# Sharing the blockwise FP4 rounding of two weight matrices between VectorE and GpSimd, beside an attention

## The reference

```python
def fp4_quant_dequant(x):                      # blocks of 16 along the last dim
    xb = x.reshape(shape[:-1] + (shape[-1] // 16, 16))
    scale = jnp.maximum(jnp.max(jnp.abs(xb), -1, keepdims=True) / 6.0, 1e-12)
    idx = jnp.searchsorted(_MID, jnp.abs(xb / scale))
    return (_GRID[idx] * jnp.sign(xb) * scale).reshape(shape)
gate = fp4_linear(x, w_gate); y = fp4_linear(x, w_up)
h = silu(gate) * y;           out = fp4_linear(h, w_down)
```

## Time and profile before

| | |
|---|---|
| median of three runs | 1594.88 us (1593.48 to 1599.5) |
| the profiled execution | 1599.5 us, its span 1597.7 us |
| busy over the span | PE 1452.7, DVE 711.7, ACT 496.5, POOL 430.0 us |
| mean granted TensorE clock | 0.934 |

### The profile page before, as it was taken

One profiled execution on the slowest core, in us unless ns is written; L12 is line 12 of the kernel. 1 busy time (PEld: TensorE's weight loads), 2 busy tenths in 40 slices (PEclk: granted clock), 3 DMA queues, 4 the chain that ended last, 5 costly groups with the idle time before them and its releaser, 6 DMA issues. The chain is left out here.

```text
span 1597.7 us, 26548 instructions
## 1 busy us (share of the span) xinstructions
PE 1452.7 (91%) x11152; PEld 1066.0 (67%) x11152; DVE 711.7 (45%) x1289; ACT 496.5 (31%) x824; POOL 430.0 (27%) x252
## 2 busy tenths in 40 slices
PE   7788987577997999999999999999999998898995
PEld 3565875243543778878878788787887876334873
DVE  2355259999524433232332323323233232675832
ACT  0313312141111204324343242432534344332602
POOL 6102010046314033313133131331313211224921
PEclk9778967788997999999999999999999999899997
DMA  6300030010201421111111011110111113203000
GB/s 246 124 35 1 1 145 1 0 73 1 79 0 60 136 75 42 54 38 47 54 37 54 31 54 54 35 55 28 59 54 35 47 39 148 106 0 125 1 1 26
DMA packets 49141, 88.01 MB, mean 55 GB/s; under 512 B 28536, under 2 KB 41088, under 8 KB 45952
## 3 DMA queue, kind: packets, MB, share of 16 engines
q1 hardware_dynamic: 49024, 86.32, 15.4%
HBM read 76.61 MB, written 9.70 MB: 54 GB/s over the span
## 5 line engine op out<-in xcount | busy, mean ns | idle before, releaser
L1151 POOL TENSOR_TENSOR ctx_hi<-ctx_raw,one 128x1536 fp32r<-128x1536 f32 (+1 forms) x32 | 91.5, 2858 | 568.7 <-DMA ctx_raw<-in_ctx 365.6
L1349 ACT COPY ET<-PS 128x512 f32<-128x512 f32 (+1 forms) x224 | 129.6, 584 | 279.8 <-PE PS L1253 204.9
L1452 DVE TENSOR_SCALAR_CACHE_REDUCE E<-PS 128x384 f32<-128x384 f32 (+1 forms) x256 | 131.8, 571 | 178.8 <-PE PS L1230 178.2
L1421 DVE TENSOR_TENSOR V<-PS,vbias 128x512 f32<-128x512 f32 (+1 forms) x104 | 71.7, 691 | 195.1 <-PE PS L1197 195.0
L1197 PE MATMUL PS<-wv_lo,ctx_hi 128*128 128x512 f32 (+1 forms) x416 | 128.4, 409 | 0.0
L1197 PE MATMUL PS<-ctx_raw_r,wk_hi 128*128 128x384 f32 (+1 forms) x512 | 128.2, 355 | 0.0
L1253 PE MATMUL PS<-ident,E 128*128 128x128 f32 (+1 forms) x832 | 123.7, 274 | 1.1 <-issue 1.1
L1356 ACT ACTIVATE E<-E,peak 128x1601 f32<-128x1601 f32 x64 | 103.5, 1623 | 66.9 <-DVE peak L1457 66.9
L1197 PE MATMUL PS<-wv_hi,ctx_hi 128*128 128x512 f32 (+1 forms) x416 | 121.3, 413 | 0.8 <-issue 0.8
L1197 PE MATMUL PS<-ctx_hi,wk_hi 128*128 128x384 f32 (+1 forms) x512 | 120.5, 357 | 0.0
L1154 POOL TENSOR_TENSOR ctx_raw_r<-ctx_raw,ctx_hi 128x1536 fp32r<-128x1536 f32 (+1 forms) x32 | 116.8, 3651 | 2.5
(11 more groups left out here) (289 smaller groups left out, 2289.9 us busy)
## 6 DMA issues: line engine op xcount, KB each, us to landing
ctx_raw<-in_ctx SPq DMA_DIRECT2D x24, 768.0 KB, 4.3
ctx_raw<-in_ctx_first SPq DMA_DIRECT2D x8, 900.0 KB, 4.6
rel_scr<-rel_out SPq DMA_DIRECT2D x8, 640.0 KB, 3.6
fwk<-in_fwk SPq DMA_DIRECT2D x1, 4096.0 KB, 12.2
fwv<-in_fwv SPq DMA_DIRECT2D x1, 4096.0 KB, 13.7
corr<-rel_scr SPq DMA_DIRECT2D x64, 48.0 KB
p_scr<-E SPq DMA_DIRECT2D x16, 192.0 KB, 2.3
near<-p_scr SPq DMA_DIRECT2D x64, 48.0 KB
```

Of the source, the lines that this page charges most:

```text
L1151: nc.gpsimd.tensor_tensor(ctx_hi[r][:, :, 0:n], ctx_raw[r][:, :, 0:n], one[:].unsqueeze(1).broadcast_to([P, KC, n]), ALU.mult).then_inc(S[ ...
L1349: nc.scalar.copy(ET[0:n, j % ET_RING, :], src[0:n, :]).then_inc(S["et_out"], 1)
L1421: v.tensor_tensor(V[0:rows, at % V_RING, :], bank(4 + NUMBER[unit] % 2)[0:rows, :], vbias[0:rows, :], ALU.add).then_inc(S["v_out"], 1)
L1452: v.tensor_scalar(E[:, p, k0:k0 + n], bank(r)[:, 0:n], 1.0, None, ALU.mult, ALU.max, accum_out=tops[:, p, c:c + 1]).then_inc(S["s_out"], 1)
```

## The change

The rounding is divided anew. DVE keeps the maxima, the scales and the division (now with the sign unchanged). The maximum with GRID becomes an operation of its own on `grid` (`floor`); then POOL, in a new `pool`, computes q + grid and q - grid, and for the first 8 of the 16 chunks (`BY_POOL`) the product with the scale as well. For the other 8 chunks DVE takes that product (`join_by_vector`). DVE waits, before the division of chunk n, for chunk n - 4 to be joined, by whichever engine. POOL's part stands between its four bias additions and its norm steps. ACT's part is as it was.

```diff
--- before.py
+++ after.py
@@ -396,7 +396,7 @@
                     residual(t - 1)
                 other(2)
             if beside:
-                beside.finish(dve, ch)
+                beside.finish(dve)
 
             dve.wait_ge(p_ready, NT)
             for t in range(NT - 1):
@@ -433,6 +433,8 @@
         def _(pool):
             for t in range(NT):
                 nc.gpsimd.tensor_tensor(s.X[:, t, :], s.X[:, t, :], s.bias[out_bias][:], ALU.add).then_inc(xb_ready, 1)
+            if beside:
+                beside.pool(pool)
             for t in range(NT):
                 nm.pool(pool, t)
 
@@ -612,17 +614,20 @@
 
     WIDTH = INNER // 2
     CHUNKS = 2 * IC * D // WIDTH
+    BY_POOL = CHUNKS // 2
     STAGES = 4
     GRID = 2.0 ** 22 + 1.0
 
     def __init__(self, nc, sem, region, s):
-        self.nc, self.s, self.started, self.measured = nc, s, 0, 0
+        self.nc, self.s, self.started, self.measured, self.floored, self.joined = nc, s, 0, 0, 0, self.BY_POOL
         nb = self.WIDTH // BLOCK
         self.q = [region.tensor(f"fp4w_q{r}", [P, self.WIDTH]) for r in range(self.STAGES)]
         self.grid = [region.tensor(f"fp4w_grid{r}", [P, self.WIDTH]) for r in range(self.STAGES)]
         self.scale = [region.tensor(f"fp4w_scale{r}", [P, 2, nb]) for r in range(self.STAGES // 2 + 1)]
         self.inverse = region.tensor("fp4w_inverse", [P, 2, nb])
-        self.divided, self.sized = sem("fp4w_divided"), sem("fp4w_sized")
+        self.divided, self.sized, self.ready, self.rounded, self.done = (
+            sem("fp4w_" + n) for n in ("divided", "sized", "ready", "rounded", "done"))
+        self.joined_dve = sem("fp4w_joined_dve")
 
     def chunk(self, n):
         w = self.s.w["wg" if n < self.CHUNKS // 2 else "wu"][:].rearrange("p r n -> p (r n)")
@@ -632,44 +637,57 @@
     def scale_of(self, n):
         return self.scale[n // 2 % len(self.scale)][:, n % 2]
 
+    def wait_joined(self, eng, n):
+
+        if n < self.BY_POOL:
+            eng.wait_ge(self.done, n + 1)
+        else:
+            eng.wait_ge(self.joined_dve, n - self.BY_POOL + 1)
+
     def vector(self, dve, ch, count):
 
         v = self.nc.vector
         for n in range(self.started, min(self.started + count, self.CHUNKS), 2):
             if n % (self.CHUNKS // 2) == 0:
                 dve.wait_ge(self.s.loaded["wg" if n == 0 else "wu"], 16)
+            if n >= 2 * len(self.scale):
+                for k in range(2):
+                    self.wait_joined(dve, n + k - 2 * len(self.scale))
             for k in range(2):
                 ch.add(v.tensor_reduce(self.scale_of(n + k), self.chunk(n + k), AX.X, ALU.max, apply_absolute_value=True))
             ch.sync()
             sc, inv = self.scale[n // 2 % len(self.scale)][:], self.inverse[:]
             ch.link(v.tensor_scalar(sc, sc, float(np.float32(1 / 6)), 1e-12, ALU.mult, ALU.max))
             ch.link(v.reciprocal(inv, sc))
-            ch.link(v.tensor_scalar(inv, inv, -(1.0 - 2.0 ** -23), None, ALU.mult))
+            ch.link(v.tensor_scalar(inv, inv, 1.0 - 2.0 ** -23, None, ALU.mult))
+            self.floor(dve, n)
+            self.join_by_vector(dve, n - 2)
             for k in range(2):
+                if n + k >= self.STAGES:
+                    self.wait_joined(dve, n + k - self.STAGES)
                 v.tensor_tensor(blocks(self.q[(n + k) % self.STAGES][:]), self.chunk(n + k),
                                 inv[:, k].unsqueeze(2).broadcast_to([P, self.WIDTH // BLOCK, BLOCK]), ALU.mult).then_inc(self.divided, 1)
             self.started = n + 2
-            if n >= 2:
-                self.complete(dve, ch, n - 2)
-
-    def complete(self, dve, ch, n):
-
-        v, pair = self.nc.vector, (n, n + 1)
-        q, grid = (lambda k: self.q[k % self.STAGES][:]), (lambda k: self.grid[k % self.STAGES][:])
-        for k in pair:
-            dve.wait_ge(self.sized, k + 1)
-            ch.add(v.scalar_tensor_tensor(q(k), grid(k), self.GRID, q(k), ALU.max, ALU.add))
-        ch.sync()
-        for k in pair:
-            ch.add(v.scalar_tensor_tensor(q(k), grid(k), self.GRID, q(k), ALU.max, ALU.subtract))
-        ch.sync()
-        for k in pair:
-            ch.add(self.join(v, k))
-        ch.sync()
-
-    def finish(self, dve, ch):
-
-        self.complete(dve, ch, self.CHUNKS - 2)
+
+    def floor(self, dve, end):
+
+        for n in range(self.floored, end):
+            grid = self.grid[n % self.STAGES][:]
+            dve.wait_ge(self.sized, n + 1)
+            self.nc.vector.tensor_scalar(grid, grid, self.GRID, None, ALU.max).then_inc(self.ready, 1)
+        self.floored = max(self.floored, end)
+
+    def join_by_vector(self, dve, end):
+
+        for n in range(self.joined, end):
+            dve.wait_ge(self.rounded, 2 * n + 2)
+            self.join(self.nc.vector, n).then_inc(self.joined_dve, 1)
+        self.joined = max(self.joined, end)
+
+    def finish(self, dve):
+
+        self.floor(dve, self.CHUNKS)
+        self.join_by_vector(dve, self.CHUNKS)
 
     def scalar(self, act, count):
 
@@ -683,6 +701,18 @@
 
         return ops.tensor_tensor(self.chunk(n), blocks(self.q[n % self.STAGES][:]),
                                  self.scale_of(n).unsqueeze(2).broadcast_to([P, self.WIDTH // BLOCK, BLOCK]), ALU.mult)
+
+    def pool(self, pool):
+
+        for n in range(self.CHUNKS):
+            q, grid = self.q[n % self.STAGES][:], self.grid[n % self.STAGES][:]
+            pool.wait_ge(self.ready, n + 1)
+            self.nc.gpsimd.tensor_tensor(q, q, grid, ALU.add).then_inc(self.rounded, 1)
+            pool.wait_ge(self.rounded, 2 * n + 1)
+            self.nc.gpsimd.tensor_tensor(q, q, grid, ALU.subtract).then_inc(self.rounded, 1)
+            if n < self.BY_POOL:
+                pool.wait_ge(self.rounded, 2 * n + 2)
+                self.join(self.nc.gpsimd, n).then_inc(self.done, 1)
 
 
 def fp4_layer(nc, sem, s, nm, after):
```

## The result

The changed kernel takes 1604.24 us in the median (1603.49 to 1605.72, four runs), the one before beside it 1594.18. The ratio is 1.0057, interval 1.0034 to 1.0081: 9 us slower, where 11 were forecast. The profiled execution took 1608.64 us, its span is 1606.8.

What follows compares the result with a forecast made beforehand. DVE's queue was taken to bound the second small attention. POOL's 70.1 us plus 14.9 lost in turns and 12.5 starving, from 233.5 to 331.0, gave +11: 1594.9 + 11 = 1606 us, range 1590 to 1615.

Steps and rivals of the forecast that it cites:

- DVE bounds the stage: Second small attention, 208 to 326 us: DVE's unbroken queue, busy 103.7 of 118 us, sets its end and the kernel's.
- DVE's work falls by 27 us: Same stage: 35.6 us of fused operations and products leave DVE, sixteen clamps of 8.4 us in all come on.
- POOL's price: 40 POOL operations of 704 elements at 1.68 us, repeated scale costed as plain: 67.0 us, 70.1 with gaps of 0.08.
- Turns: In the stage, DVE and POOL operations on SBUF block each other and alternate; POOL loses 14.9 us.
- The early start of 0.14 us: A held operation starts 0.14 us before the other engine's recorded end; with 0 instead, the walk ends 8 us later.
- the prediction's walk: Stepping four engines' program order through the stage with estimated durations; stage ends 10.9 us later, walk against walk.
- the rival of full holds: Each turn in the stage lasts both whole recorded durations: +19 us, 1614 us; chance 0.08.
- The clamps: Sixteen new DVE maxima with GRID, 0.53 us each, 8.4 in all; the profile would show two kinds, 0.53 and near 2.
- The rival of cheaper turns: Only some DVE operations in the stage, such as products, take turns with POOL: no change, about 1598 us; chance 0.25.
- Starving: POOL waits in the stage for clamps that come late: 12.5 us in five gaps, the largest 5.7.
- The ends: POOL runs from 233.5 to 331.0 us; the stage ends 10.9 to 12.3 us later, taken as +11.
- The faster rival: POOL and DVE run side by side without turns; the stage ends 13 to 14 us sooner, 1581 us; chance 0.13.

Runs made afterwards that it cites:

- e2: Changed kernel with POOL's additions, subtractions and products on only the first 16 of 704 elements; 1570.9 us, ratio 0.9849 to the kernel before.
- e5: Kernel before, with seven of sixteen products with the scale on POOL, of even chunks 0 to 12; 1594.5 us, ratio 1.0006 to before.
- e1: Changed kernel with DVE's division and product with the scale replaced by one-input reductions of the same shape; 1582.9 us, ratio 0.9926 to the kernel before.
- e6: Kernel before, with nine products with the scale on POOL (chunks 1, 2, 3, 5, 6, 7, 9, 10, 11); 1584.6 us, ratio 0.9945 to before.
- e7: Changed kernel with no product with the scale on POOL, all 16 on DVE; 1618.6 us, ratio 1.0160 to the kernel before.
- e8: Changed kernel with 12 of 16 products with the scale on POOL in place of 8; 1603.9 us in one run.
- e3: Kernel before, with 40 added POOL multiplications of 512 elements on a tensor nobody reads any more; 1616.0 us in one run.
- e4: Kernel before, with seven of sixteen products with the scale on POOL, of odd chunks 1 to 13; 1587.4 us, ratio 0.9955 to before.

## Why the prediction held, step by step

**DVE bounds the stage, the stage passes to the end undiminished.** Held: +10.6 in the stage of the profiled executions, 9 to 10 in the times. In the eight experiments the kernel's time moved by what the stage moved, within 2.5 us.

**DVE's work falls by 27 us.** Held as work. In time it is worth 21.5 us (e2); the forecast gave no price for it with POOL out of the way.

**POOL's price.** 1.68 was forecast for all forty; additions and subtractions measured 1.66 to 1.67, the product with the repeated scale 1.38 to 1.39. That the repeated scale costs what a plain operand does was wrong, by 0.29 x 8 = 2.3 us. POOL's own work is 32 x 1.67 + 8 x 1.39 = 64.6 us where 67.0 were taken.

**Turns.** The 40 operations last 79.0 us together, so 79.0 - 64.6 = 14.4 us are lost to DVE, forecast 14.9. One term of that was wrong by its own rule: behind the softmax product of 1.23 a POOL operation loses 1.23 - 0.36 = 0.87, not 1.07, and the two so held took 2.53 and 2.54 in place of 1.67. That softmax shift and residual go free was assumed without a row; they do (1.23 at 245.97, 0.68 at 255.48). The early start of 0.14 us before the other's recorded end holds at this size: in e5 POOL's product ends at 238.63, DVE's operation behind it at 239.37, which less its own 0.89 is 238.48. By the prediction's walk, turns that lasted both whole durations would have put the stage 8 us later; the rival of full holds is gone. The Trainium skill (SBUF — State Buffer, Who interferes with whom) names the pairs of operations rightly, and e1 bears out its other half, that a DVE instruction with one SBUF input outside the two-port modes goes beside POOL freely.

**The clamps.** The forecast had two kinds, 0.53 and near 2 us. Measured: one of sixteen was held that long, the last, at 1.71; most pairs stand at 0.96, as POOL was already idle when they came. The rival of cheaper turns is gone all the same: the division with a repeated factor takes its turn (2.35), and so does the scaling (1.53). Nor do DVE's back-to-back operations go first: a pair of divisions takes 4.65 with POOL's operations between.

**Starving.** Forecast 12.5 us, measured 15.4 (gaps before the operations at 251, 262, 277, 289, 300, 314 and 324 us; the largest 5.7, as forecast). The small ones before 262 and 289 were missing in the forecast; POOL's products there end 0.1 us before the clamps come, and cost 0.29 less than forecast. What the product's price gave, starving took.

**The ends.** POOL began 10.5 us after DVE's second softmax (235.79 - 225.33), forecast 10.1. Its last subtraction ends 96.5 us after its first addition begins; forecast 97.5; the difference is in the 0.08 us between operations, which was charged 39 times, though eight operations start without it. I had taken 11 us for the shift, between 10.9 and 12.3. Counted from the second softmax on DVE, which TensorE's faster first scores (3.76 us) brought 2.1 us forward, the stage grew from 103.2 to 115.9 us, 12.7. So the upper end was nearer the truth for the stage, and the first scores gave 2 us back. The forecast has no term for that, so agreement owes 2 us to luck. The first scores stand ahead of every edit; they took 3.76 us in the changed kernel, e1, e6, e7 and e8, and 5.3 to 5.4 in the one before, e2, e3, e4 and e5, and no run shows why. That two errors of 2 to 3 us, in the product's price and in the starving, cancelled was luck too. The mechanism was right all the same. The median moved by 9 to 10 us, less than the stage's 10.6; the difference is within the interval and isn't explained further.

**The faster rival**, no turns, would have been 1581 us (its sum gives POOL's end as 305.4, not 305.8). e1, which frees the divisions and products and leaves 5 us of turns in, stands at 1582.9.

## What to carry to other kernels

Before work goes from DVE to POOL, sort both engines' operations by whether they need both inputs from SBUF (or are a DVE tensor_scalar): those of one engine hold those of the other, and POOL's are nearly twice as long. Then ask what stands behind a held operation and who waits for it: in e7 the work of both fell by 4 us and the stage grew by 12. Give POOL pieces that are released just as DVE turns to reductions, moments or operands in PSUM, and no longer than those last: seven or nine of sixteen small products so placed gained 7 and 10 us, where seven placed one operation earlier gained none, and the forty operations of the change cost 10. A busy time that doesn't fall when work is taken away is a sign of held operations; the least and the median duration of one form, side by side, show it.

## What the runs showed of the hardware

POOL's tensor_tensor depends on its operands: 704 elements with two full inputs 1.67 us, with the second input repeated 16 times in its innermost dimension 1.39; 512 elements with two different inputs 1.27, with the same tensor twice 1.04. A reduction over a dimension of one moves 704 elements on DVE in 0.87 us, as long as a product, and takes no turn with POOL. Where both engines had a queue in the changed kernel's stage, they alternated one operation each (DVE's pairs at 4.64 us with POOL's 2.20 and 1.92 between).
